# A fused convolution and linear attention: order of the queries' loop, and the planes' edges on VectorE

## The chip, the cores and the metric

The kernel runs on one core of a Trainium2 chip. The metric is the time of one execution on the device in microseconds (us); three runs of the kernel before gave a median of 4165.56 (4163.43 to 4168.52). The engines are TensorE (PE; its weight loads are PEld), VectorE (DVE), ScalarE (ACT), GpSimd (POOL) and SyncE (SP), which issues the DMAs.

## The reference

The input x is (16, 256, 64, 64) in float32. Layer 0 is a group norm and a 3x3 convolution in 8 groups, with weights rotated per batch by an angle that a small network takes from the pooled input, and a modulation per channel. Layer 1 is a group norm and a focused linear attention with 8 heads over the 4096 pixels, with a 5x5 depthwise convolution of the values:

```python
x = x + conv(gn(x), rotated) * sigmoid(mod)
t = tokens(gn(x))
q, k, v = t @ Wq.T + bq, t @ Wk.T + bk, t @ Wv.T + bv
q, k = (relu(q) + 1e-6) / scale, (relu(k) + 1e-6) / scale
q = q ** 3 / norm(q ** 3) * norm(q)              # k likewise; then split into 8 heads
z = 1 / (q @ k.sum(tokens) + 1e-6)
o = (q @ (k.T @ v)) * z + depthwise5x5(v)
x = x + (o @ Wproj.T + bproj)
```

## The kernel before

The program is one loop over the 16 batches b, written out per engine; each engine runs its own list of instructions in order, and counters (semaphores) hold one back until another has done its part. Within a batch come five stages: keys and values (a unit is 512 pixels, a pair is 256 pixels or two tiles of 128; `step_kv`), the state k.T @ v, the depthwise convolution of V (`depthwise`, 32 channels), the 3x3 convolution of batch b + 1 (`convolution`, 8 groups, each in two halves q = 0 and 1 into the two banks of VA), and the queries of batch b (`step_q`). The last two batches are written out apart; the last has no convolution.

**The queries' loop** has NU = 8 units of two pairs, p = 0 and 1. Pair n = 2u + p goes through a chain over all engines:

- TensorE `project` (line 1283, bias 1285) into the bank F[p]; VectorE `floor_max` (809) in place; ScalarE `squares` (1079), two activations with their sums; VectorE `cube` (815) into K3; ScalarE `sixths` (1085); VectorE `ratio` (820, 823); ScalarE `norms` (1091).
- TensorE `transpose_q` (1333) from K3 into the bank T[0]; ScalarE `transposed_q` (1126) copies it to QT; TensorE `attention` (1342) into both banks of VA; VectorE `denominators`, `inverses`, `quotients` (869, 874, 883) into O; GpSimd `add_depthwise` (528).
- TensorE `transpose_o` (1351) into the bank T[1]; ScalarE `high_out` (1130), the high half of O in float16; VectorE `low_out` (899), the rest. With both pairs of a unit there, TensorE `output` (1361) makes both halves of the channels in the banks PP and SM, VectorE `finish` (893) adds the residual, and SyncE stores.

TensorE's step takes its parts of different pairs, in this order:

```python
if live(p):
    pe.wait_ge(f_cube, b * 2 * PAIRS + PAIRS + 2 * u + p + 1)
    project(b, u, p, F, 0)
if live(p - 1):
    transpose_q(b, u - 1 + p, 1 - p)
if live(p - 2):
    attention(b, u - 1, p)
if p == 1 and live(-4):
    for h in range(HALVES):
        output(b, u - 2, h)
if live(p - 3):
    transpose_o(b, u - 2 + p, 1 - p)
```

`live` says whether such a pair exists. `attention` waits for QT of its pair and for the quotients of the pair before; `transpose_o` for O of its pair (o_rdy) and for low_out of the pair before (ol_rdy); `output` for low_out of both pairs of its unit and for `finish` of the unit before. In the same loop SyncE, ScalarE, VectorE and GpSimd take in the next batch (`attn_input`, lines 1070, 803, 519), and in units 8 and 9 TensorE projects the keys and values of its first unit.

**The planes.** The 3x3 convolution reads four planes of 33 x 34 elements per group, whose edges have to be 0. ScalarE `planes` normalises one group's planes in place (1056) and then writes the edges by two activations of 64 x 34 and four of 32 x 32 elements with scale 0 (1061, 1064); the counter cx_rdy tells VectorE `high` (775), which casts the planes to float16, and GpSimd takes the rest (511). Groups 0 to 2 are made during `depthwise`, behind the evacuations (1119) of channels 20, 24 and 28; groups 3 to 7 during `convolution`. There VectorE calls `high` for group g + 3 once the second half of group g is in its bank, ahead of that half's evacuation (792) and statistics (795).

## Time and profile before

| | |
|---|---|
| Runs | 4165.56 us median of 3 (4163.43 to 4168.52) |
| The profiled execution | 4166.2 us, its span 4164.4 us |
| Busy: PE, PEld | 3627.7 us (87%), 2717.4 us (65%) |
| Busy: DVE, ACT, POOL | 2896.2 (70%), 2871.0 (69%), 1394.6 (33%) |
| One batch, middle of the run | 249.2 us, 98.8 of them the queries' loop |
| Largest waits of PE in the loop over batches | for DVE line 830: 59.5 us; for DVE line 899: 54.1; for DVE line 815: 52.4; for ACT line 1119: 47.1 |
| Largest waits of DVE | for ACT line 1064: 288.7 us; for PE line 1264: 243.4; for ACT line 1085: 150.2; for ACT line 1130: 108.9 |
| ACT's edges, all batches | line 1061: 58.9 us in 256 instructions; line 1064: 133.8 us in 512 |

How to read it: busy time is the sum of an engine's instructions, and matmuls are pipelined, so that what a matmul costs its successors is the distance between starts. A row in order of time has the start, the length, engine and line, the operation, out<-in, how many instructions are merged, and in brackets how long the engine was idle before it and what released it. PEclk is the granted clock of TensorE: 1.00 is 2.4 GHz, 0.50 is 1.2 GHz.

### The profile page before, as it was taken

The page shows a single profiled execution, that of the slowest core. Times are in us where ns is not written, and L with a number is a line of the kernel's source. Part 1 is how long each engine was busy: PE and PEld are TensorE (multiplying, and loading weights), DVE is VectorE, ACT ScalarE, POOL GpSimd, SP SyncE. Part 2 cuts the span into 40 slices and gives each one's busy share as a digit, 9 for nine tenths or more (in the row PEclk, how much of TensorE's full clock was granted, in tenths as well). Part 3 has the DMA queues.
Part 4 walks back from the last instruction along what each step waited for, and adds up shares of the span by engine and source line. Part 5 has one row for each costly group of instructions (what it writes and reads, how often), then busy time and mean ns, then how long its engine had stood idle before and what let it go on. Part 6 is the DMA issues. An engine that isn't in the chain of part 4 may idle for free.

```text
span 4164.4 us, 94153 instructions
## 1 busy us (share of the span) xinstructions
PE 3627.7 (87%) x26496; PEld 2717.4 (65%) x26496; DVE 2896.2 (70%) x7633; ACT 2871.0 (69%) x8141; POOL 1394.6 (33%) x1317
## 2 busy tenths in 40 slices
PE   0468999989989988999989989988999989989998
PEld 0155776757667675776757667675766757667676
DVE  6465867768586775867768586785867668585766
ACT  2376776767677676776767677676777767677675
POOL 0441523325133241523325143342523325143311
PEclk9989999999999999999999999999999999999999
DMA  4435434344443435434344443535434344442512
GB/s 164 139 98 155 135 104 132 124 119 141 128 131 107 134 113 155 134 109 135 117 124 140 126 140 96 144 105 154 134 115 137 109 132 132 129 139 59 152 46 72
DMA packets 558467, 516.39 MB, mean 124 GB/s; under 512 B 97296, under 2 KB 491664, under 8 KB 557712
## 3 DMA queue, kind: packets, MB, share of 16 engines
q1 hardware_dynamic: 557968, 510.53, 40.7%
q8 instruction: 217, 3.56, 0.4%
q14 instruction: 282, 2.31, 0.2%
HBM read 351.02 MB, written 134.22 MB: 117 GB/s over the span
## 4 chain that ended last, share of the span: by engine, by line
PE 59%; DVE 16%; issue 11%; ACT 10%; DMA 1%; DVEq 1%; POOL 1%; SPq 1%; ACTq 0%; POOLq 0%
PE VAB L1264 17%; PE F L1283 10%; PE VAB L1283 6%; PE F L1322 5%; PE T L1294 4%; PE VAB L1322 4%; PE SM L1361 4%; PE VAB L1342 2%; ACT WK L1085 2%; ACT WK L1079 2%; DVE WK L830 2%; PE T L1351 2%; DVE F L809 2%; ACT V L1119 2%; PE F L1285 2%
## 5 line engine op out<-in xcount | busy, mean ns | idle before, releaser
L1283 PE MATMUL F<-WQ,XHL 128*128 128x256 f16 x6144 | 814.0, 273 | 47.1 <-DVE XR L792 13.7
L1264 PE MATMUL VAB<-WK,BD 128*128 128x512 f16 x3072 | 724.9, 395 | 103.4 <-DMA BD<-RHL 54.7
L528 POOL TENSOR_TENSOR XR<-XR,V 128x512 f32<-128x512 f32 x256 | 327.5, 1279 | 1226.6 <-DVE XR L883 1226.6
L1079 ACT ACTIVATE WK<-F,SCAL 128x256 f32<-128x256 f32 x1024 | 474.3, 469 | 369.1 <-DVE F L809 368.3
L511 POOL TENSOR_TENSOR WK<-XP,WK 128x1122 f16<-128x1122 f32 x128 | 289.9, 2265 | 1248.1 <-DVE WK L775 1248.1
L1283 PEld LDWEIGHTS F<-WQ,XHL 128*128 128x128 f16 (+1 forms) x6144 | 600.3, 99 | 124.5 <-issue 56.0
L1264 PEld LDWEIGHTS VAB<-WK,BD 128*128 128x128 f16 x3072 | 302.5, 101 | 492.3 <-issue 87.7
L1085 ACT ACTIVATE WK<-WK,SCAL 128x256 f32<-128x256 f32 x1024 | 513.0, 508 | 66.2 <-DVE WK L815 62.7
L809 DVE TENSOR_TENSOR F<-F,FL 128x512 f32<-128x512 f32 x512 | 354.7, 693 | 86.9 <-PE F L1285 85.1
L815 DVE TENSOR_TENSOR WK<-WK,F 128x512 f32<-128x512 f32 x512 | 349.6, 683 | 88.2 <-ACT WK L1079 73.7
L1283 PE MATMUL VAB<-WQ,XHL 128*128 128x256 f16 x3072 | 407.0, 273 | 0.0
L792 DVE SCALAR_TENSOR_TENSOR XR<-VAB,MODC,XR 128x512 f32<-128x512 f32 x256 | 191.7, 749 | 243.8 <-PE VAB L1264 243.4
L1156 ACT ACTIVATE XR<-XR,BPC 128x1024 f32<-128x1024 f32 x128 | 146.9, 1147 | 304.5 <-DVE ST L795 304.3
L1294 PE MATMUL T<-VT,WK 128*128 128x129 f32 x2048 | 295.2, 289 | 66.5 <-DVE WK L830 59.5
L775 DVE CAST WK<-XP 128x1122 f16<-128x1122 f32 x128 | 97.3, 762 | 352.4 <-ACT XP L1064 288.7
L1283 PEld LDWEIGHTS VAB<-WQ,XHL 128*128 (+1 forms) x3072 | 301.4, 98 | 36.3
L1294 PEld LDWEIGHTS T<-VT,WK 128*128 128x128 f32 x2048 | 261.2, 199 | 94.0 <-DVE WK L830 88.8
L519 POOL TENSOR_TENSOR XHL<-XP,XHL 128x512 f16<-128x512 f32 x256 | 291.2, 1139 | 93.2 <-DVE XHL L803 93.2
L1342 PE MATMUL VAB<-KVS,VT 128*128 128x132 f32 x2048 | 300.0, 292 | 21.2 <-DVE XR L883 16.4
L1322 PE MATMUL F<-V,TP 128*128 128x248 f16 (+1 forms) x2304 | 297.5, 286 | 14.1 <-ACT V L1119 14.1
L1342 PEld LDWEIGHTS VAB<-KVS,VT 128*128 128x128 f32 x2048 | 261.3, 197 | 52.2 <-DVE XR L883 46.7
L1285 PE MATMUL F<-BQ,ONES 128*128 128x256 f16 x1024 | 279.8, 273 | 0.0
(185 smaller groups left out, 7128.2 us busy)
## 6 DMA issues: line engine op xcount, KB each, us to landing
XR<-xr SPq DMA_DIRECT2D x256, 512.0 KB, 4.9
XP<-xp SPq DMA_DIRECT2D x128, 561.0 KB, 3.8
x<-XR SPq DMA_DIRECT2D x512, 128.0 KB, 2.1
XP<-x SPq DMA_DIRECT2D x256, 256.0 KB, 3.4
XR<-x SPq DMA_DIRECT2D x256, 256.0 KB, 3.3
out<-XR SPq DMA_DIRECT2D x256, 256.0 KB, 3.0
BD<-RHL SPq DMA_DIRECT2D x256, 96.0 KB, 2.3
XHL<-toeplitz SPq DMA_DIRECT2D x2, 3072.0 KB, 12.8
```

The lines of the kernel that those rows point to most:

```text
L519: g_.tensor_tensor(lo, U[:, u % 3, h].rearrange("p m y x -> p y m x"), hi, ALU.subtract).then_inc(l_rdy, 1)
L528: g_.tensor_tensor(o, o, fm, ALU.add).then_inc(o_rdy, 2)
L809: v.tensor_tensor(f, f, fl, ALU.max).then_inc(f_max, 1)
L815: v.tensor_tensor(K3[:, p, :], K2[:, p, :], F[p][:, :], ALU.mult).then_inc(f_cube, 1)
L1079: a.activation(K2[:, p, ts], F[p][:, ts], ACT.Square, scale=inv_a, accum_out=S2[:, 2 * p + t:2 * p + t + 1]).then_inc(f_sq, 1)
L1085: a.activation(K2[:, p, t * C:(t + 1) * C], K3[:, p, t * C:(t + 1) * C], ACT.Square, scale=inv_a, accum_out=S6[:, 2 * p + t:2 * p + t + 1] ...
L1264: ins = t_.matmul(VA[q], BD[:, j, HALVES * wa + h, sx, P * sy:P * (sy + 1)], SG[:, g % 3, xa, 16 * q + sy:16 * q + sy + 16, sx:sx + 32], s ...
L1283: t_.matmul(o, XHL[:, xa, h, at], WQ[:, wa, h, c0:c0 + C], start=(k == 0), stop=False)
L1285: ins = t_.matmul(o, ONES[:, :], BQ[:, c0:c0 + C], start=False, stop=True)
L1294: ins = t_.matmul(T[h][:, 0:P + 1], K3[:, p, t * C + h * P:t * C + (h + 1) * P], VT[:, p, t, h, 0:P + 1], start=False, stop=False)
L1322: ins = t_.matmul(bank[:, lo:hi], TP[:, c, d, ta, :], V[:, c, va, lo + sh:hi + sh], start=(k == 0), stop=(k == 8))
L1342: ins = t_.matmul(VA[t][:, h * KVC:(h + 1) * KVC], QT[:, p, h, t * P:(t + 1) * P], KVS[:, h, :], start=True, stop=True)
```

## The change

Three engines get another order in `step_q`, and VectorE makes the edges of the planes.

- TensorE: attention, transposes of O, projection (or keys of the next batch), transposes of Q; then output of unit u - 2, if p = 0 instead of p = 1. Values of the next batch come last in both steps of unit 9.
- VectorE: denominators, inverses and quotients of pair n - 2 come first, then floor and ratio, low_out of pair n - 3 (was n - 4), both finishes of unit u - 2 at p = 1 (was one per step, of unit u - 3), cube.
- ScalarE: high_out of pair n - 3 comes first in each step (was both of a unit in steps with p = 0); squares, norms, transposed_q, attn_input and sixths keep their order.
- The edges: the six activations are gone from `planes`; `high` waits for the normalised planes (cx_main), issues six memsets and waits for them (cx_rdy).

```diff
@@ VectorE
             def high(c, g):
-                dve.wait_ge(cx_rdy, GROUPS * c + g + 1)
+                dve.wait_ge(cx_main, GROUPS * c + g + 1)
+                s = g % 3
+                for p in range(2):
+                    v.memset(XG[64 * p:64 * p + 64, s, 32 * p, :], 0.0).then_inc(cx_rdy, 1)
+                for p in range(4):
+                    v.memset(XG[32 * p:32 * p + 32, s, 1 - p // 2:33 - p // 2, 32 * (p % 2)], 0.0).then_inc(cx_rdy, 1)
+                dve.wait_ge(cx_rdy, 6 * (GROUPS * c + g + 1))
...
             def step_q(b, u, p, live, nxt, keys=False, fresh=False):
                 n = b * 2 * PAIRS + PAIRS + 2 * u + p
-                if live(p - 4):
-                    low_out(b, u - 2, p)
+                if live(p - 2):
+                    denominators(b, u - 1, p)
+                    inverses(b, u - 1, p)
+                    quotients(b, u - 1, p, fresh and u == 1 and p == 0)
                 if live(p) or keys:
                     floor_max(n, p)
...
-                if live(-6):
-                    finish(b, u - 3, p)
-                if live(p - 2):
-                    denominators(b, u - 1, p)
+                if live(p - 3):
+                    low_out(b, u - 2 + p, 1 - p)
+                if p == 1 and live(-4):
+                    for h in range(HALVES):
+                        finish(b, u - 2, h)
                 if live(p) or keys:
                     cube(n, p)
-                if live(p - 2):
-                    inverses(b, u - 1, p)
-                if live(p - 2):
-                    quotients(b, u - 1, p, fresh and u == 1 and p == 0)
@@ ScalarE
-                act.wait_ge(cx_main, GROUPS * c + g + 1)
-                for p in range(2):
-                    edge = XG[64 * p:64 * p + 64, s, 32 * p, :]
-                    a.activation(edge, edge, ACT.Copy, scale=0.0)
-                for p in range(4):
-                    edge = XG[32 * p:32 * p + 32, s, 1 - p // 2:33 - p // 2, 32 * (p % 2)]
-                    ins = a.activation(edge, edge, ACT.Copy, scale=0.0)
-                ins.then_inc(cx_rdy, 1)
...
-                if p == 0 and live(-4):
-                    high_out(b, u - 2, 0)
+                if live(p - 3):
+                    high_out(b, u - 2 + p, 1 - p)
                 if live(p) or keys:
                     squares(n, p)
...
-                if p == 0 and live(-3):
-                    high_out(b, u - 2, 1)
@@ TensorE
-            def step_q(b, u, p, live):
+            def step_q(b, u, p, live, nxt):
+
+                if live(p - 2):
+                    attention(b, u - 1, p)
+                if live(p - 3):
+                    transpose_o(b, u - 2 + p, 1 - p)
                 if live(p):
                     pe.wait_ge(f_cube, b * 2 * PAIRS + PAIRS + 2 * u + p + 1)
                     project(b, u, p, F, 0)
+                elif nxt and u == NU:
+                    keys(b + 1, 0, p)
                 if live(p - 1):
                     transpose_q(b, u - 1 + p, 1 - p)
-                if live(p - 2):
-                    attention(b, u - 1, p)
-                if p == 1 and live(-4):
+                if p == 0 and live(-4):
                     for h in range(HALVES):
                         output(b, u - 2, h)
-                if live(p - 3):
-                    transpose_o(b, u - 2 + p, 1 - p)
+                if nxt and u == NU + 1:
+                    if p == 0:
+                        pe.wait_ge(o_rdy, 2 * PAIRS * (b + 1) + O_CR)
+                        carry(pe)
+                    values(b + 1, 0, p)
```

The first place is TensorE in a unit in the middle of the queries' loop. T<-MATS,WK are the transposes of Q, T<-MATS,XR those of O, VAB<-KVS,VT is attention, PP and SM are output; an ISA or REGISTER_ALU row is an instruction that only carries a wait. Before, second step of a unit from its projection on:

```order
L1283 MATMUL F<-WQ,XHL 128x256 [waits f_cube]
...
L1330 REGISTER_ALU [waits f_cube]
L1333 MATMUL T<-MATS,WK 128x128 [waits qt_rdy]
...
L1339 ISA [waits qt_rdy]
L1342 MATMUL VAB<-KVS,VT 128x132 [waits z_rdy]
...
L1361 MATMUL PP<-XR,WP 128x512 [waits y_rdy]
...
L1351 MATMUL T<-MATS,XR 128x128 [waits ol_rdy,o_rdy]
```

And now, a step with p = 0:

```order
L1333 ISA [waits qt_rdy]
L1336 MATMUL VAB<-KVS,VT 128x132 [waits z_rdy]
...
L1345 MATMUL T<-MATS,XR 128x128 [waits ol_rdy,o_rdy]
...
L1277 MATMUL F<-WQ,XHL 128x256 [waits f_cube]
...
L1327 MATMUL T<-MATS,WK 128x128 [waits qt_rdy,f_cube]
...
L1351 ISA [waits ol_rdy]
L1355 MATMUL PP<-XR,WP 128x512 [waits y_rdy]
```

The attention and the transposes of O have moved from behind the projection to ahead of it, and output stands last, ahead of the next step's attention.

The second place is ScalarE in the same units: XR<-T is high_out, WK<-F squares, NORM norms, VT<-T the copy to QT, XP attn_input, WK<-WK sixths. Before, a step with p = 0, from its high_out to that of the step's end:

```order
L1130 ACTIVATE XR<-T,SCAL 128x2x256 [waits ot_full]
...
L1079 ACTIVATE WK,S<-F,SCAL 128x256 [waits f_six]
...
L1091 ACTIVATE NORM<-RATIO,SCAL 128x2 [waits f_ratio]
L1126 COPY VT<-T 128x512 [waits cube_used]
...
L1130 ACTIVATE XR<-T,SCAL 128x2x256 [waits ot_full]
L1085 ACTIVATE WK,S<-WK,SCAL 128x256 [waits f_cube]
```

And now, a step:

```order
L1127 ACTIVATE XR<-T,SCAL 128x2x256 [waits ot_full]
...
L1073 ISA [waits f_cube,f_max]
L1076 ACTIVATE WK,S<-F,SCAL 128x256 [waits f_six]
...
L1088 ACTIVATE NORM<-RATIO,SCAL 128x2 [waits f_ratio]
L1123 COPY VT<-T 128x512 [waits cube_used]
...
L1082 ACTIVATE WK,S<-WK,SCAL 128x256 [waits f_cube]
```

One high_out stands ahead of the squares in every step; the copy to QT stands behind the squares of the next pair, as before.

## Rows read from the trace of the kernel before

**Rows 1.** PE, PEld, DVE, ACT, POOL busy by stretch of one queries' loop; clock, DMA
```profile
1144.99:1154.63 9.64, 6.68 (x54) 5.21 (x55) 5.89 (x24) 6.94 (x19) 0.00 (x0) 1.00 0.44 125
1154.63:1229.11 74.48, 69.66 (x517) 54.41 (x515) 63.06 (x182) 55.43 (x174) 28.80 (x24) 0.98 0.43 124
1229.11:1243.75 14.64, 10.90 (x68) 6.70 (x68) 12.92 (x25) 9.78 (x25) 8.29 (x8) 1.00 0.58 172
```

**Rows 2.** TensorE in order of time (start, length, instruction), in the same loop
```profile
1170.92 1.46 PE L1361 MATMUL PP<-XR,WP 128*128 128x512 f16 x6
...
1173.51 0.60 PE L1351 MATMUL T<-MATS,XR 128*128 128x128 f32 x4
...
1193.28 0.60 PE L1351 MATMUL T<-MATS,XR 128*128 128x128 f32 x4
...
1193.72 0.82 PE L1283 MATMUL F<-WQ,XHL 128*128 128x256 f16 x6
...
1195.69 1.07 PE L1342 MATMUL VAB<-KVS,VT 128*128 128x132 f32 x8
...
1196.59 0.60 PE L1351 MATMUL T<-MATS,XR 128*128 128x128 f32 x4
...
1203.24 0.60 PE L1351 MATMUL T<-MATS,XR 128*128 128x128 f32 x4
```

**Rows 3.** All engines in order of time; in brackets the idle time before, and releaser
```profile
1153.46 0.57 ACT L1126 COPY VT<-T 128x512 f32<-128x512 f32 x1
...
1154.17 0.63 PE L1333 MATMUL T<-MATS,WK 128*128 128x128 f32 x4 [2.06 <-ACT VT L1126]
...
1195.59 0.69 DVE L809 TENSOR_TENSOR F<-F,FL 128x512 f32<-128x512 f32 x1
...
1196.40 0.47 ACT L1079 ACTIVATE WK<-F,SCAL 128x256 f32<-128x256 f32 x1 [1.51 <-DVE F L809]
...
1196.63 0.74 DVE L893 SCALAR_TENSOR_TENSOR XR<-PP,SCAL,XR 128x512 f32<-128x512 f32 x1
...
1197.31 0.29 ACT L1091 ACTIVATE NORM<-RATIO,SCAL 128x2 f32<-128x2 f32 x1
...
1197.50 0.58 ACT L1126 COPY VT<-T 128x512 f32<-128x512 f32 x1
...
1236.30 0.73 DVE L899 SCALAR_TENSOR_TENSOR XR<-T,SCAL,XR 128x512 f16<-128x512 f32 x1
...
1237.18 0.63 PE L1351 MATMUL T<-MATS,XR 128*128 128x128 f32 x4 [3.47 <-DVE XR L899]
...
1246.31 0.83 PE L1283 MATMUL F<-WQ,XHL 128*128 128x256 f16 x6 [0.67 <-issue]
...
1248.04 0.70 DVE L809 TENSOR_TENSOR F<-F,FL 128x512 f32<-128x512 f32 x1 [1.13 <-PE F L1285]
```

**Rows 4.** Waits of two engines over the span (total, times, longest); depthwise's end, convolution
```profile
DVE XR L899 <- ACT XR L1130: 108.9, 129, 2.5
...
PE F L1322 <- ACT V L1119: 14.1, 30, 0.7
...
1096.63 1.01 ACT L1119 ACTIVATE V<-VAB,DWB,SCAL 128x256 f32<-128x256 f32 x2
...
1098.22 7.14 PE L1264 MATMUL VAB<-WK,BD 128*128 128x512 f16 x24 [3.13 <-ACT V L1119]
...
1127.52 5.50 PE L1264 MATMUL VAB<-WK,BD 128*128 128x512 f16 x24
```

**Rows 5.** A fill on VectorE in the setup; small instructions beside GpSimd in the convolution
```profile
1.66 0.28 DVE L573 MEMSET KVS<- 128x264 f32 x1
...
1106.49 2.32 POOL L511 TENSOR_TENSOR WK<-XP,WK 128x1122 f16<-128x1122 f32 x1 [7.07 <-DVE WK L775]
...
1107.79 1.04 DVE L699 TENSOR_TENSOR GS<-GS 128x8 f32<-128x8 f32 x1
```

**Rows 6.** TensorE behind a longer wait, early in the queries' loop
```profile
1163.99 0.71 PEld L1333 LDWEIGHTS T<-MATS,WK 128*128 128x128 f32 x4 [2.80 <-ACT VT L1126]
```

More of the change, by code:

```diff
@@ L1141, in step_q @@
                     norms(n - 1, 1 - p, den_eps)
+                    transposed_q(b, u - 1 + p, 1 - p)
                 elif keys:
                     norms(n - 1, 1 - p, inv_a2)
-                if live(p - 1):
-                    transposed_q(b, u - 1 + p, 1 - p)
                 if nxt:
                     attn_input(b + 1, u - 3, p)
-                if p == 0 and live(-3):
-                    high_out(b, u - 2, 1)
                 if live(p) or keys:
@@ L1414, in batch @@
                     for p in range(2):
-                        if not last and u == NU:
-                            keys(b + 1, 0, p)
-                        if not last and u == NU + 1 and p == 1:
-                            pe.wait_ge(o_rdy, 2 * PAIRS * (b + 1) + O_CR)
-                            carry(pe)
-                            values(b + 1, 0, 0)
-                        step_q(b, u, p, alive(u))
+                        step_q(b, u, p, alive(u), not last)
                         if not last and u == 0:
                             (group_mean, group_spread)[p](b + 1, 1)
-                if not last:
-                    values(b + 1, 0, 1)
             pe.wait_ge(ready, 1)
```

## Prediction

> **What bounds the kernel now.** I read the busy time by stage first, then TensorE's order of time in the queries' loop, then who waits for whom. In the loop's middle TensorE is busy 69.66 of 74.48 us, VectorE 63.06 [rows 1]. TensorE's records end later than they free the engine, so a better reading is its starts: one unit of the loop (two pairs of query tiles) goes from the transposes of O at 1193.28 to the same at 1203.24, 9.96 us [rows 2], and between them TensorE hardly stops. VectorE's only standing wait is the one for ScalarE's high part of O (line 899 behind line 1130), 108.9 us in all [rows 4]. So TensorE and VectorE are both nearly full, and the loop is quick because each engine finds the other's result ready. In such a loop the order on each queue is what counts, since each engine takes its instructions in order.
>
> **What the change moves.** Call step k = 2u + p. Before, TensorE's step was project(k), transpose Q(k-1), attention(k-2), output if p = 1, transpose O(k-3). So while ScalarE was still making QT of pair k-2, TensorE projected pair k. Now the step is attention(k-2), transpose O(k-3), project(k), transpose Q(k-1), output if p = 0. ScalarE keeps its order: squares(k) stands ahead of the copy QT(k-1), as the rows of order show. That closes a ring: attention(k-2), then project(k), whose bank VectorE floors, then ScalarE's squares(k), the norms, the copy QT(k-1), and only then attention(k-1). Nothing in it can run ahead, as each link is behind the one before it on its queue or waits for it.
>
> **The ring's length**, link by link:
> - attention to the transposes of O, start to start: 1196.59 - 1195.69 = 0.90 [rows 2];
> - those to the projection: 1193.72 - 1193.28 = 0.44 [rows 2];
> - projection to VectorE's floor: 1248.04 - 1246.31 = 1.73 [rows 3];
> - floor to squares: 1196.40 - 1195.59 = 0.81 [rows 3];
> - squares to norms 0.91, norms to copy 0.19 (starts 1196.40, 1197.31, 1197.50) [rows 3];
> - copy to the TensorE instruction that waits for it: 1154.17 - 1153.46 = 0.71 [rows 3].
>
> Sum 5.69 us for a step without output. VectorE's denominators, inverses and quotients, which now stand ahead of the floor, end about 2.3 us after the attention starts and the floor can start at 3.07, so they hide.
>
> In a step with p = 0, output stands between this ring and the next attention, and it waits for the low part of pair k-3, which VectorE makes in the same step after floor and ratio. Attention to floor is 0.90 + 0.44 + 1.73 = 3.07; floor to the instruction behind ratio 1196.63 - 1195.59 = 1.04 [rows 3]; low part to the TensorE instruction that waits for it 1237.18 - 1236.30 = 0.88 [rows 3]; two outputs 1173.51 - 1170.92 = 2.59 [rows 2]. Sum 7.58. A unit therefore takes 5.69 + 7.58 = 13.27 us in place of 9.96. TensorE stands still in it for about 5.69 - 3.30 = 2.4 us and once more for some 1.7 us.
>
> **A batch.** From attention(0) to attention(15) there are 15 steps: 7 with output (7 x 7.58 = 53.1), 7 without (39.8), the first one without transposes of O (5.69 - 0.44 = 5.25), and 1.5 more where VectorE does the small chain of the second group norm. Together 99.6, against 74.48 before [rows 1]: +25.1. The start, 9.64 before [rows 1], loses 0.5, since attention(0) no longer stands behind transposes that wait for QT. The end, 14.64 before [rows 1], gains about 1.5: output of unit 7 now waits within one step for the transposes, ScalarE's part (behind the last sixths) and VectorE's part, and nothing covers it; values of the next batch, which covered it, come behind. My estimate for it is 16.1, with ends of 14.6 and 19. So +26.1 a batch, and 16 batches give **+418 us**.
>
> **The fills.** During the depthwise stage ScalarE made three planes with six small instructions each. The last two evacuations start at 1096.63 and end at 1097.64, and the convolution starts at 1098.22, 3.13 us after TensorE's last matmul, which therefore ended at 1095.09 [rows 4]. Without the fills ScalarE has caught up: one evacuation (0.51) and the same 0.58 of waking remain, so about 1.1 of 3.13; saved 2.0. The waits inside the stage, 14.1 us in all [rows 4], are 0.9 a batch and go too. After the wait the first 24 matmuls take 7.14 instead of 5.50 [rows 4]; behind a wait of 1.1 they should not: 1.6. Together 4.6, for 15 batches **-69 us** (between -30, if the clock falls anyway, and -69).
>
> On VectorE, the nearest row is a memset of 264 elements, 0.28 us [rows 5]; fills of 32 or 34 elements take a third of it or less, six of them with the wait behind them some 0.65. They stand behind the wait for the convolution's second half, ahead of the cast and of the evacuation of bank 1, for which TensorE has another half in hand (5.50 / 2 = 2.75 us [rows 4]): hidden at most groups. At group 2 the small chain of the next batch's group norm follows at once, and the next evacuation was already just in time: 0.65 late, 14 batches, **+9 us** (0 to +45, if all five fills of a batch showed).
> A short VectorE instruction can take longer than its work: line 699 took 1.04 us for 8 elements while GpSimd's line 511 ran until 1108.81 [rows 5]. The Trainium skill (SBUF - State Buffer, Who interferes with whom) says that a VectorE instruction with two inputs in SBUF is blocked for the whole of a GpSimd instruction that reads SBUF, and one with at most one input, outside its two-port modes, is not. By it the fills, which read nothing, stay at their own length, and the sum is as above; if they were held like line 699, the last of them would come 1 us later each time. This trace agrees for line 699; for a fill beside GpSimd no run here shows it.
>
> **The clock.** Behind a wait of 2.52 us the transposes took 1.11 us instead of the 0.63 behind one of 2.06 [rows 3, 6]; yet behind 3.47 they took 0.63 again [rows 3]. So TensorE falls to half clock behind some such waits and not behind others. The new loop has a wait of 2.4 us in each of about 7 units. One fall costs 1.64 us by the convolution's first matmuls [rows 4]. None would be 0, all would be 7 x 16 x 1.64 = 184; I take half, **+92 us**, as 2.4 lies between the wait that did it and the one that didn't.
>
> **Sum.** 4166.2 (the profiled execution's own time, 0.6 above the median of 4165.56) + 418 - 69 + 9 + 92 = **4616 us**, 10.8% slower. Range: the clock takes 92 off or adds 92; the links can each be 0.03 to 0.05 off, 0.2 a step, 15 x 16 x 0.2 = 48 either way; the end of a batch adds up to 45. **4470 to 4770**.
>
> **Rivals.**
> - **VectorE's wait goes and nothing comes in its place** (faster). The low part is now made in the step after the transposes of O, which come early, so the 108.9 us of line 899 [rows 4] would vanish: 4166 - 109 - 69 + 9 = 3997 us. It decides if QT(k-1) is ready before project(k) is needed. What speaks for it is that VectorE works 63 of 74 us; against it, that ScalarE's copy stands behind squares(k) in both kernels. Chance 0.04.
> - **Only half of the ring closes.** If output didn't wait for the low part of its own step, both steps would take about 5.69, a unit 11.38: +1.42 x 7.5 x 16 = 170; 4166 + 170 - 60 = 4276 us. Against it is the wait on ol_rdy ahead of output, for both pairs of the unit, the second of which is k-3. Chance 0.06.
> - **TensorE stays at half clock in the loop.** Its parts of the ring, about 2 x 2.87 + 2.59 = 8.3 us a unit, would double: + 8.3 x 7.5 x 16 = 1000, 5500 us. Each slow stretch in this trace ended by itself under dense work, and the loop keeps TensorE busy over two thirds. Chance 0.03.
> - **It doesn't do what it says.** The order of the built kernel shows the steps moved on TensorE, so there is no case of no change. Near zero.
>
> **Chances.** The forecast has 0.87, the range leaves out the rivals. A difference of 0.2% is about what a measurement of this kernel can tell. Faster 0.04, same 0.01, slower 0.95.
>
> **What would show it.** Right: attention to attention 5.7 and 7.6 us in turn, TensorE's line of attention waiting for ScalarE's copy QT some 2.4 us once a unit and its output waiting for VectorE's low part some 1.7 us; the convolution's start waiting 1.1 us for ScalarE; VectorE's wait for line 1130 gone, one for attention there. Wrong: a unit under 11 us, or attention that finds QT ready.

## The result and the profile after

The changed kernel takes **4685.39 us** (median of 4 runs, 4682.73 to 4687.55), the kernel before 4165.85 beside it: ratio **1.1247**, 95% interval 1.1231 to 1.1264. I had said 4616, range 4470 to 4770. Its profiled execution has a span of 4684.2 us and a mean granted clock of 0.947, against 0.971 before.

The windows of one middle batch (us; busy time and count of PE, PEld, DVE, ACT, POOL; clock; DMA). The stretches are the start of the queries' loop, attention(0) to attention(15), end of the batch, keys and values:
```profile
1237.83:1246.99 9.16, 4.67 (x36) 3.51 (x37) 5.28 (x23) 6.46 (x17) 0.00 (x0) 0.96 0.42 117
1246.99:1350.77 103.78, 75.06 (x531) 58.90 (x532) 66.99 (x185) 58.72 (x180) 30.99 (x26) 0.95 0.33 96
1350.77:1371.39 20.62, 12.23 (x71) 7.62 (x70) 11.19 (x24) 10.18 (x24) 8.44 (x11) 0.83 0.38 111
1371.39:1436.31 64.92, 60.05 (x517) 53.07 (x517) 49.25 (x134) 52.12 (x183) 29.89 (x38) 0.97 0.28 84
```
The start is 9.16 for 9.64, as forecast. The second row answers to the 74.48 of [rows 1]: 29.3 us more, with nearly the same work in it (531 matmuls for 517; TensorE 75.06 busy against 69.66, in part because of half clock). The third answers to the end of a batch: before it was 16.24 from attention(15) to the keys' stage, now 20.62 at a clock of 0.83.

The ring in all engines' order of time (start, length, instruction, idle before and releaser), from attention(k-2) to attention(k-1):
```profile
1308.99 1.06 PE L1336 MATMUL VAB<-KVS,VT 128*128 128x132 f32 x8
1309.89 0.60 PE L1345 MATMUL T<-MATS,XR 128*128 128x128 f32 x4
...
1310.33 0.82 PE L1277 MATMUL F<-WQ,XHL 128*128 128x256 f16 x6
...
1312.06 0.70 DVE L816 TENSOR_TENSOR F<-F,FL 128x512 f32<-128x512 f32 x1 [0.71 <-PE F L1279]
...
1312.88 0.47 ACT L1076 ACTIVATE WK<-F,SCAL 128x256 f32<-128x256 f32 x1 [1.66 <-DVE F L816]
...
1313.79 0.29 ACT L1088 ACTIVATE NORM<-RATIO,SCAL 128x2 f32<-128x2 f32 x1
...
1313.97 0.58 ACT L1123 COPY VT<-T 128x512 f32<-128x512 f32 x1
```
Attention to floor 3.07 us, floor to squares 0.82, squares to norms 0.91, norms to copy 0.18, and 0.71 to the next attention at 1314.68: 5.69, link by link as the prediction has it.

TensorE around it (attention L1336, transposes of O L1345, project L1277, transpose Q L1327, output L1355):
```profile
1301.29 1.16 PE L1336 MATMUL VAB<-KVS,VT 128*128 128x132 f32 x8 [2.23 <-ACT VT L1123]
...
1306.39 1.47 PE L1355 MATMUL PP<-XR,WP 128*128 128x512 f16 x6 [1.54 <-DVE XR L906]
1307.70 1.46 PE L1355 MATMUL SM<-XR,WP 128*128 128x512 f16 x6
...
1314.68 2.12 PE L1336 MATMUL VAB<-KVS,VT 128*128 128x132 f32 x8 [2.23 <-ACT VT L1123]
1316.60 1.06 PE L1345 MATMUL T<-MATS,XR 128*128 128x128 f32 x4
1317.45 1.09 PE L1277 MATMUL F<-WQ,XHL 128*128 128x256 f16 x6
```
Two waits a unit. A step with output takes 7.70 (1301.29 to 1308.99), one without 5.69. The wait of 2.23 is followed once by full clock (1.16; granted clock 1.00 from 1301.29 to 1304.26) and once by half (2.12, and 1.06 and 1.09 behind it, where 0.60 and 0.82 are usual; granted clock 0.50 from 1314.68 to 1317.9). The waits over the span, by TensorE, VectorE and ScalarE (total, times, longest):
```profile
PE VAB L1336 <- ACT VT L1123: 333.6, 144, 3.6
PE PP L1355 <- DVE XR L906: 228.0, 128, 3.8
DVE Z L876 <- PE VAB L1336: 333.2, 163, 3.8
DVE XR L906 <- ACT XR L1127: 14.0, 16, 0.9
```
VectorE's wait for ScalarE's high part, 108.9 us in [rows 4], is down to 14.0, as rival 1 had said; in its place TensorE waits 333.6 us for the copy QT and 228.0 for the low part.

The end of the batch, TensorE:
```profile
1355.77 0.63 PE L1345 MATMUL T<-MATS,XR 128*128 128x128 f32 x4 [1.97 <-DVE XR L906]
1360.16 2.74 PE L1355 MATMUL PP<-XR,WP 128*128 128x512 f16 x6 [3.76 <-DVE XR L906]
1362.69 2.77 PE L1355 MATMUL SM<-XR,WP 128*128 128x512 f16 x6
...
1371.39 0.28 PE L1388 MATMUL T<-NOT,ONES 32*128 32x130 f16 x2 [2.65 <-issue]
1372.41 1.30 PE L1277 MATMUL F<-WQ,XHL 128*128 128x256 f16 x6 [0.74 <-issue]
```
The last output waits 3.76 us and then runs at half clock (2.74 for 1.47; granted clock 0.50 from 1360.2 to 1365.2), and most of the next stage's first projection is at half clock too (1.30 for the 0.83 of [rows 3]).

### The profile page after: what moved, and what is told of

It reads as the page before. It is cut to its first block, busy times and chain, and to the rows that moved or that the text cites. A ratio compares the mean times of both kernels' runs of the same rounds, so it can differ in the third digit from the quotient of the medians.

```text
span 4684.2 us, 94247 instructions
## 1 busy us (share of the span) xinstructions
PE 3734.0 (80%) x26496; PEld 2796.9 (60%) x26496; DVE 2981.2 (64%) x8401; ACT 2702.0 (58%) x7373; POOL 1400.1 (30%) x1317
## 4 chain that ended last, share of the span: by engine, by line
PE 60%; DVE 17%; issue 10%; ACT 9%; DVEq 1%; DMA 1%; POOL 1%; SPq 0%; ACTq 0%; POOLq 0%
PE F L1277 12%; PE VAB L1258 10%; PE VAB L1336 6%; PE F L1316 5%; PE VAB L1277 5%; PE VAB L1316 5%; PE PP L1355 4%; PE SM L1355 4%; ACT WK L1076 4%; PE T L1288 3%; DVE F L816 3%; PE T L1345 2%; PE F L1279 2%; DVE XR L906 2%; DVE XR L799 2%
## 5 line engine op out<-in xcount | busy, mean ns | idle before, releaser
L1277 PE MATMUL F<-WQ,XHL 128*128 128x256 f16 x6144 | 874.6, 286 | 45.8 <-DVE XR L799 13.7
L1258 PE MATMUL VAB<-WK,BD 128*128 128x512 f16 x3072 | 707.9, 386 | 85.3 <-DMA BD<-RHL 54.7
L1277 PEld LDWEIGHTS F<-WQ,XHL 128*128 128x128 f16 (+1 forms) x6144 | 628.7, 103 | 149.3 <-issue 54.8
L1336 PE MATMUL VAB<-KVS,VT 128*128 128x132 f32 x2048 | 322.3, 306 | 333.6 <-ACT VT L1123 333.6
L1258 PEld LDWEIGHTS VAB<-WK,BD 128*128 128x128 f16 x3072 | 291.2, 98 | 466.7 <-DMA BD<-RHL 54.8
L1336 PEld LDWEIGHTS VAB<-KVS,VT 128*128 128x128 f32 x2048 | 288.8, 209 | 382.7 <-issue 325.8
L1277 PE MATMUL VAB<-WQ,XHL 128*128 128x256 f16 x3072 | 410.8, 275 | 0.0
L1355 PE MATMUL PP<-XR,WP 128*128 128x512 f16 x768 | 207.6, 411 | 228.0 <-DVE XR L906 228.0
L1277 PEld LDWEIGHTS VAB<-WQ,XHL 128*128 (+1 forms) x3072 | 305.2, 99 | 43.3 <-issue 7.7
L1127 ACT ACTIVATE XR<-T,SCAL 128x512 f16<-128x512 f32 x256 | 174.0, 680 | 264.7 <-PE T L1345 264.7
L1094 ACT ACTIVATE V<-VAB,SCAL 128x256 f32 (+1 forms) x512 | 214.6, 470 | 139.0 <-PE VAB L1279 133.1
```

Of the source, the lines that this page charges most:

```text
L1258: ins = t_.matmul(VA[q], BD[:, j, HALVES * wa + h, sx, P * sy:P * (sy + 1)], SG[:, g % 3, xa, 16 * q + sy:16 * q + sy + 16, sx:sx + 32], s ...
L1277: t_.matmul(o, XHL[:, xa, h, at], WQ[:, wa, h, c0:c0 + C], start=(k == 0), stop=False)
L1336: ins = t_.matmul(VA[t][:, h * KVC:(h + 1) * KVC], QT[:, p, h, t * P:(t + 1) * P], KVS[:, h, :], start=True, stop=True)
L1355: ins = t_.matmul((PP, SM)[h][:, :], WP[:, wa, kk, h * P:(h + 1) * P], OT[:, xa, kk, :].rearrange("p (y m x) -> p m y x", y=4, m=4), start ...
```

## The experiments

Stages of all kernels, each the mean of the 14 middle batches, worked out from TensorE's starts in the trace of each (us a batch; "times 16" below turns one into a sum over the run; keys includes the end of the state, depthwise runs to the convolution's first matmul, the next column holds the convolution and the start of the queries' loop, end runs from attention(15) to the keys' stage):

| kernel | keys | depthwise | convolution to attention(0) | loop | end | time of the runs, ratio to before |
|---|---|---|---|---|---|---|
| before | 65.2 | 36.9 | 56.2 | 74.4 | 16.0 | 4165 to 4167 |
| changed | 66.5 | 33.8 | 55.7 | 105.7 | 19.9 | 4685.4, 1.1247 |
| fills only | 66.0 | 33.6 | 56.2 | 74.4 | 17.0 | 4140.4, 0.9933 (0.9919 to 0.9946) |
| order only | 66.5 | 36.9 | 55.8 | 104.2 | 19.6 | 4716.3, 1.1319 (1.1301 to 1.1336) |
| copy ahead | 66.8 | 33.1 | 52.8 | 100.5 | 18.9 | 4544.3, 1.0902 (1.0885 to 1.0918) |
| output late | 66.3 | 33.3 | 55.7 | 99.3 | 16.4 | 4528.2, 1.0856 (1.0837 to 1.0874) |
| output late, busy | 66.8 | 33.0 | 55.7 | 90.7 | 14.9 | 4371.1, 1.0497 (1.0478 to 1.0516) |
| attention first | 66.6 | 36.6 | 55.6 | 108.0 | 17.7 | 4740.2, 1.1378 (1.1358 to 1.1399) |
| both first | 65.1 | 36.5 | 55.6 | 98.5 | 16.4 | 4539.9, 1.0889 (1.0870 to 1.0908) |
| new order | 66.5 | 36.7 | 54.2 | 71.6 | 16.1 | 4113.8, 0.9873 (0.9857 to 0.9888) |
| fills early | 66.3 | 33.4 | 55.0 | 74.8 | 16.9 | 4125.4, 0.9889 (0.9873 to 0.9906) |
| new order, early | 67.2 | 33.3 | 52.9 | 72.2 | 15.8 | 4051.5, 0.9724 (0.9710 to 0.9737) |
| fills, busy end | 65.4 | 33.1 | 56.2 | 74.5 | 16.0 | 4114.4, 0.9872 (0.9855 to 0.9889) |
| new, early, busy end | 66.9 | 33.2 | 52.9 | 72.5 | 15.2 | 4032.7, 0.9682 (0.9665 to 0.9698) |

**The two halves apart.** Fills only: the kernel before, with the changed kernel's `high` and `planes`. Order only: the changed kernel with `high` and `planes` of before.

> The kernel before, with the edges of the planes filled by VectorE and no order changed. My theory: what ScalarE gets back in the depthwise stage is the prediction's -69 (4.6 us a batch), and the fills, six of which the changed kernel's trace shows to take 0.96 us from the first to the cast, cost VectorE nothing but at the group with the small chain: +9 to +15. So 4166 - 69 + 9 to 15 = 4106 to 4115 us, the convolution starting 1.1 to 1.2 us after the last depthwise copy is waited for. Rival: in the convolution VectorE is the engine waited for, so that every one of five groups comes 1 us later: the gain would be at most 2.0 to 4.6 - 5 x 0.96 = about 0, 4155 to 4170 us.

> The changed kernel, with the edges back on ScalarE as before: the order alone. If the parts add up, it is slower than the changed kernel by what the fills gain, 50 to 70 us: 4735 to 4755 us, 1.137 to 1.142 of the time before; the loop of queries takes 103.8 us a batch as in the changed kernel. Rival: part of the gain of the fills is taken back by a clock that falls elsewhere, then under 30 us between them: 4700 to 4715 us.

Fills only gives -27, half of what I expected; order only is 31 above the changed kernel, about the rival's figure of under 30: its loop is 1.5 us a batch shorter than the changed kernel's, where the clock falls more often. So the loss is the order's alone, and the fills are worth 27 to 31, not 60. The table says where the rest went: depthwise gives 3.3 us a batch (2.9 forecast), but the convolution takes as long as before, although its first matmuls no longer run at half clock, and end and keys take 1.8 more. The convolution in fills only, TensorE:
```profile
1105.33 8.26 PE L1262 MATMUL VAB<-WK,BD 128*128 128x512 f16 x36 [0.20 <-DVE XR L798]
1113.86 0.39 PE L1228 MATMUL SM<-SB,MATS 128*128 128x8 f32 x2 [0.26 <-DVE SB L718]
1114.56 2.85 PE L1262 MATMUL VAB<-WK,BD 128*128 128x512 f16 x12 [0.32 <-DVE XR L798]
1117.60 2.85 PE L1262 MATMUL VAB<-WK,BD 128*128 128x512 f16 x12 [0.20 <-DVE XR L798]
```
and its VectorE:
```profile
1096.91 0.24 DVE L775 MEMSET XP<- 64x34 f32 x2 [1.31 <-PE VAB L1262]
1097.23 0.61 DVE L777 MEMSET XP<- 32x32 f32 x4
1097.87 0.75 DVE L781 CAST WK<-XP 128x1122 f16<-128x1122 f32 x1
```
The six fills and the step to the cast take 0.96 us (1096.91 to 1097.87), and TensorE waits for VectorE's evacuations at several groups. Over the span the wait of the convolution for the evacuation is:
```profile
PE VAB L1262 <- DVE XR L798: 12.4, 44, 2.1
```
In the kernel before it is 1.3 us, one time.

**Fills early.** Only the place of the fills is new; `edges(c, g)` holds the six of a group:
```diff
                         v.bn_stats(ST[:, 1, g, q, :], tile).then_inc(s1_rdy, 1)
+                        if q == 0 and g + 3 < GROUPS:
+                            edges(c, g + 3)
```


> The kernel with only the fills on VectorE, but each group's fills behind the statistics of the first half of the group three earlier, where TensorE has another half to do, instead of ahead of the cast. The run with the fills alone gained 27 us where I expected 51 to 60; its trace starts the convolution 3.3 us earlier, has 5.51 us for the first 24 matmuls, and yet ends the stage no sooner: TensorE waits 0.2 to 0.3 us for VectorE's evacuations at several groups. My theory: those waits are the fills' 0.96 us ahead of cast and evacuation; off that chain the convolution gets its 1.6 us a batch back: 4110 to 4120 us, and the stage from its first matmul to the first attention 54.5 to 55.0 in place of 56.2. Rival (the fills' work itself is too much for VectorE there, or the loss is the clock's): the stage stays at 56.0 to 56.4 and the time at 4135 to 4145 us.

The stage fell to 55.0, as forecast, and the wait above is down from 12.4 to 4.7 us. The time, 4125, is 5 over the range (two of the five runs lie in it): the loop took 0.4 and the keys 0.3 us a batch more. So the fills ahead of the cast cost 1.2 us a batch. That is the first half of what was missing.

**Busy end.** The other half should be the clock. In the kernel before, the wait of 3.47 at a batch's end is followed by full clock [rows 3], in all 13 middle batches that have it (the 14th waits 3.22, and its clock falls in both kernels). In fills only, the same wait in the same place is followed by half clock in 10 of the 13. One of them:
```profile
1230.25 0.63 PE L1349 MATMUL T<-MATS,XR 128*128 128x128 f32 x4 [3.46 <-DVE XR L905]
...
1231.48 1.46 PE L1281 MATMUL VAB<-WQ,XHL 128*128 128x256 f16 x6
1232.73 0.42 PE L1283 MATMUL VAB<-BQ,ONES 128*128 128x256 f16 x1
1232.94 2.43 PE L1359 MATMUL PP<-XR,WP 128*128 128x512 f16 x6
```
The second projection and most of the output are at half clock (granted clock 0.54 from 1231.5 to 1235.2; it is 1.00 behind the wait in the kernel before). The kernel "fills, busy end" fills that wait (the result is read by nobody):
```diff
+                if u == NU + 1 and p == 0:
+                    pe.wait_ge(qt_rdy, b * PAIRS + PAIRS + QT_CR)
+                    for _ in range(26):
+                        t_.matmul(T[0][:, 0:C], ONES[:, :], BQ[:, 0:C], start=True, stop=True)
```


> The run with the fills alone, plus 26 matmuls of 256 columns whose result nobody reads, ahead of the last transposes of O of a batch, where TensorE waits 3.46 us for VectorE. In the kernel before that wait is followed by full clock, in the run with the fills alone by half clock in most batches, though it is as long; the end of the batch took 0.96 us more and the keys' stage 0.82 more. My theory (the fills' gain was given back as falls of the clock there): with TensorE busy in the wait the end of a batch is back at 16.0 or less, 1.0 to 1.8 us a batch less: 4111 to 4125 us. Rival (the loss there is not the clock's, or the fall only moves to the next wait): 4135 to 4145 us.

```profile
1220.57 3.00 PE L1369 MATMUL T<-BQ,ONES 128*128 128x256 f16 x26
1224.21 0.63 PE L1349 MATMUL T<-MATS,XR 128*128 128x128 f32 x4 [0.64 <-DVE XR L905]
```
4114.4: another 26 us gone, the end back at 16.0. TensorE has more work and the kernel is faster; behind the shorter wait its rows are at full clock (granted clock 1.00 from 1224.2 to 1228.5) in all 14 batches. With it the fills are worth 50 us, near the 60 of the prediction (whether the same matmuls would help the kernel before, whose end is at full clock already, was not run). In [rows 4] the convolution's first matmuls were at half clock; the edit took that fall away, and falls came at the end of the batch. Why the end's wait is followed by full clock in one kernel and mostly by half in the other, no run tells.

**The ring, link by link.** Copy ahead changes one place of ScalarE in the changed kernel:
```diff
+                if live(p - 1):
+                    transposed_q(b, u - 1 + p, 1 - p)
                 if live(p) or keys:
                     squares(n, p)
                 if live(p - 1):
                     norms(n - 1, 1 - p, den_eps)
-                    transposed_q(b, u - 1 + p, 1 - p)
```


> The changed kernel, with ScalarE's copy QT(k-1) ahead of squares(k) instead of behind its norms: this opens the ring at the link that the prediction names, and leaves TensorE's and VectorE's orders alone. My theory: the step without output goes from 5.69 to about 4.2 us (attention, transposes of O, project, transpose Q, copy, 0.9 + 0.4 + 1.3 + 0.6 + 0.9), the step with output stays at 7.6 to 8.5, because that one waits for the low part of O, so a unit takes 11.8 to 12.7 in place of 13.39: 7.5 x 16 x 0.7 to 1.6 = 84 to 190 us less, 4495 to 4600 us. TensorE's wait for QT is mostly gone, the one for the low part is longer. Rival (the loss is TensorE's own, by the half clock or by order of banks, not by the copy): steps of 5.69 and 7.70 stay and the time stays within 10 us of 4685.

-141 us, inside the range. In the loop the step without output takes 4.22 in every batch, TensorE's wait for the copy falls from 333.6 to 95.3 us, and the wait for the low part grows:
```profile
PE PP L1356 <- DVE XR L906: 298.1, 128, 3.8
PE VAB L1337 <- ACT VT L1123: 95.3, 129, 1.0
```
The step with output has grown from 7.70 to 8.49, or 10.17 where the clock falls behind that wait. So the copy's place behind squares(k) sets the short step, and the low part the long one. The loop gives 5.1 us a batch, 82 of the 141 us. Another 46 come ahead of it: from the first projection to attention(0) a batch takes 6.2 us in place of 9.0, since the first copy no longer stands behind squares either; 16 come at the end.

Output late moves the second link, with a second buffer for the parts of O. TensorE's part is below; VectorE's finish comes one step later too:
```diff
-                if p == 0 and live(-4):
+                if p == 1 and live(-4):
                     for h in range(HALVES):
                         output(b, u - 2, h)
```


> The changed kernel, with output of unit u-2 one step later (end of the step p = 1) and the sums of it in VectorE one step later too; the high and low parts of O get a second buffer. So output no longer waits for a low part of its own step and fills the time in which TensorE waits for QT. My theory: both steps are the ring alone, 5.7 to 5.9 us, a unit 11.4 to 11.7 in place of 13.39, 7.5 x 16 x 1.7 to 2.0 = 204 to 240 us less: 4445 to 4485 us; TensorE's wait for the low part is gone, that for QT 2.2 us only in every second step. If the falls of the clock go with the wait, up to 50 less. Rival (the second wait only takes its share of one that would come anyway, as for the copy): unit over 12.8, less than 70 us gained.

-157 us, less than the 204 forecast. Steps of 5.69 and 5.99 are there as the ring says, and the wait for the low part is gone, but in most units the longer step takes 7.66. TensorE in one of them:
```profile
1268.45 1.66 PE L1336 MATMUL VAB<-KVS,VT 128*128 128x132 f32 x8 [2.23 <-ACT VT L1123]
1269.91 1.06 PE L1345 MATMUL T<-MATS,XR 128*128 128x128 f32 x4
1270.76 1.49 PE L1277 MATMUL F<-WQ,XHL 128*128 128x256 f16 x6
```
The same 2.23 us as in the changed kernel, now followed by half clock (granted clock 0.57 from 1268.45 to 1272.0) in mostly four or five of the six steps with output; in the changed kernel it is one or two of seven. To show that it is the clock, the same kernel with work in that wait:
```diff
+                if p == 0 and live(-1):
+                    pe.wait_ge(z_rdy, 4 * (b * PAIRS + 2 * (u - 1) + 1) + Z_CR)
+                    for _ in range(12):
+                        t_.matmul(VA[0][:, 0:C], ONES[:, :], BQ[:, 0:C], start=True, stop=True)
```


> The run with output late, plus 12 matmuls of 256 columns whose result nobody reads, in the step p = 0 behind transpose Q, where TensorE waits 2.2 us for QT. They add 1.3 us of work to a wait and no work to the path. In the run without them 5 of 7 units a batch had a step of 7.66 instead of 5.99, the rest at half clock. My theory (those steps are the clock's answer to the wait): with the wait under 1 us the steps of 7.66 are gone, a unit takes 5.69 + 5.99 = 11.7, 5 x 1.67 x 16 = 130 us less: 4390 to 4420 us, mean granted clock over 0.96 in place of 0.934. Rival (the longer step has another cause, such as VectorE or a port, or the clock falls whatever TensorE does): 4500 to 4560 us, steps of 7.66 as before.

```profile
1233.43 1.47 PE L1377 MATMUL VAB<-BQ,ONES 128*128 128x256 f16 x12
1235.75 1.17 PE L1336 MATMUL VAB<-KVS,VT 128*128 128x132 f32 x8 [0.84 <-ACT VT L1123]
1236.75 0.60 PE L1345 MATMUL T<-MATS,XR 128*128 128x128 f32 x4
```
-157 us, 19 below the range: steps of 5.61 and 6.00, none of 7.66 from the fourth on, clock 0.969. The loop gives 138 us of it, close to the 130 expected; the end, which I had not counted, gives 23. The falls are the price of the wait, and work that nobody reads buys them off.

**Which move closes the ring.** Attention first is the kernel before with one move on TensorE:
```diff
+                if live(p - 2):
+                    attention(b, u - 1, p)
                 if live(p):
                     pe.wait_ge(f_cube, b * 2 * PAIRS + PAIRS + 2 * u + p + 1)
                     project(b, u, p, F, 0)
                 if live(p - 1):
                     transpose_q(b, u - 1 + p, 1 - p)
-                if live(p - 2):
-                    attention(b, u - 1, p)
```


> The kernel before with one move on TensorE alone: attention(k-2) ahead of project(k) and transpose Q(k-1); output stays where it was, in the step p = 1, so it never waits for a low part of its own step. My theory (the ring closes by this one move): a step without output 5.69 - 0.44 = 5.25 us, a step with output TensorE's own 3.30 + 2.59 = 5.9 us, a unit 11.1 to 11.2 without a fall of the clock, 12.8 with one in every unit (1.66 each, as in the run with output late): 4166 + 7.5 x 16 x 1.2 to 2.9 = 4310 to 4510 us. Rival (it takes both moves to close the ring, attention first alone finds QT ready since ScalarE has a step more): unit 10.0 to 10.4, 4170 to 4220 us.

4740 us, slower than the changed kernel and far above both ranges. It is no ring by ScalarE's copy. VectorE, and TensorE behind it:
```profile
1264.43 0.70 DVE L809 TENSOR_TENSOR F<-F,FL 128x512 f32<-128x512 f32 x1 [6.46 <-PE F L1285]
...
1267.28 0.76 DVE L883 TENSOR_TENSOR XR<-VAB,Z 128x256 f32<-128x256 f32 x2
...
1268.09 1.73 PE L1342 MATMUL VAB<-KVS,VT 128*128 128x132 f32 x8 [2.84 <-DVE XR L883]
```
VectorE has the floor of pair k and its cube ahead of the quotients of pair k-2. As attention(k-2) now precedes project(k), those quotients wait for a projection that they don't need, and the next attention waits for them to free its bank. Both first puts denominators, inverses and quotients ahead of the floor:
```diff
+                if live(p - 2):
+                    denominators(b, u - 1, p)
+                    inverses(b, u - 1, p)
+                    quotients(b, u - 1, p, fresh and u == 1 and p == 0)
                 if live(p) or keys:
                     floor_max(n, p)
```


> The run with attention first on TensorE alone (4740 us, where I had expected 4310 to 4510), and in VectorE the denominators, inverses and quotients of pair k-2 ahead of the floor of pair k, as the changed kernel has them. In that run's trace every step takes 6.39 us: VectorE floors project(k) first, and the quotients that free attention's bank come behind it. My theory: with them first only ScalarE's copy closes the ring: 5.25 us without output, 5.9 with, a unit 11.1 to 11.3, 12.8 with a fall of the clock in each: 4310 to 4510 us, VectorE's quotients no longer waited for by attention. Rival (the order of attention and projection on TensorE costs this much in any company): over 4650 us.

-200 us, 4540. TensorE's attention waits for the copy alone (354.1 us, none listed for the quotients). It is 30 over my range: steps are 5.64 and 6.60 (7.99 with a fall) where I had 5.25 and 5.9, because VectorE's low part now waits 181.9 us for ScalarE's high part ahead of the quotients:
```profile
PE VAB L1340 <- ACT VT L1124: 354.1, 160, 3.6
DVE XR L899 <- ACT XR L1128: 181.9, 203, 2.8
```
So attention first is what closes the ring, and VectorE's move is a repair without which it costs 200 us more. Order only is another 176 us slower than both first. Output in the step of its own low part can be most of that (moving it gave 157 us in output late); the transposes of O ahead of the projection and the new places of the high and low parts were not run apart.

**A version that beats both.** New order keeps project(k) first on TensorE and takes attention(k-2) ahead of transpose Q(k-1), output ahead of the transposes of O; in VectorE the quotients of a unit's second pair stand behind the cube, and the sums of output frame the step p = 0. `ratio` and `attn_input` get other places too, `attn_input` ahead of squares on ScalarE; no run tells these moves apart. The copy's place in ScalarE's step:
```diff
                 if live(p) or keys:
                     squares(n, p)
+                if live(p - 1):
+                    transposed_q(b, u - 1 + p, 1 - p)
+                if p == 0 and live(-3):
+                    high_out(b, u - 2, 1)
                 if live(p - 1):
                     norms(n - 1, 1 - p, den_eps)
```


> The kernel before with the queries' step rearranged in another way: TensorE projects pair k first, as before, then takes attention(k-2), transpose Q(k-1), output, transposes of O; ScalarE copies QT(k-1) right behind squares(k), ahead of the norms; VectorE ends the unit with the quotients of the second pair. Fills stay on ScalarE. My theory (an engine that projects k first has work of its own while QT is being made, so the link that the changed kernel closes stays open, and moving the copy up makes it earlier still): the unit falls from 9.96 to 9.2 to 9.6 us, 7 x 16 x 0.36 to 0.76 = 40 to 85 us less, 4080 to 4127 us. Rival (attention ahead of transpose Q is what costs, wherever the projection stands): QT(k-1) comes later, the unit grows to 10.5 us or more, over 4220 us.

> Both of the two before in one kernel (new order in the queries' loop, fills on VectorE and early). If they add up: 4080 to 4127 less 27 to 55, 4030 to 4095 us, faster than both the kernel before and the changed one. Rival: falls of the clock take back what one of them gains, as they took about half of it in the run with the fills alone: then within 15 us of the better of the two.

New order: -53 us. TensorE's starts in its trace:
```profile
1186.62 1.07 PE L1352 MATMUL VAB<-KVS,VT 128*128 128x132 f32 x8
1187.52 0.60 PE L1343 MATMUL T<-MATS,WK 128*128 128x128 f32 x4
...
1189.92 1.07 PE L1352 MATMUL VAB<-KVS,VT 128*128 128x132 f32 x8
```
Steps of 3.30 and 5.90 in turn, a unit of 9.20 against 9.96 [rows 2], with no wait of TensorE left in its middle. The loop gives 2.9 us a batch and the stretch from the first projection to attention(0) another 2.0 (the copy to QT stands ahead of squares, as in copy ahead); the keys' stage takes 1.4 back. With early fills 4051.5, 62 less, where the fills early alone brought 41. And with the busy end:

> The run with both the new order and the early fills (4051 us), plus the same 26 matmuls in the wait at the end of a batch. Its keys' stage takes 67.2 us a batch against 65.2 of the kernel before, with the same work. My theory: half to all of these 2 us are falls of the clock that the wait brings: 4020 to 4040 us. Rival: the fall moves on to the next wait: 4045 to 4058 us.

4032.7, **0.9682 of the time before**, inside the range; but the keys' stage stayed at 66.9 and the end fell by 0.5 only, so my reason for it holds for a part: the two traces differ by 9 us, the medians by 19, as the trace is one of two runs at 4041 and 4042, with the other three at 4031 to 4033. In the trace the end is at full clock in every batch, but the first projection of the keys takes 2.8 to 3.0 us in 7 of the 14 batches (2.2 to 3.0 in 13 of them without the busy end), where the kernel before has 1.54 in all. In the mean that is 0.7 of the 1.7 us by which the keys' stage is longer here than before; the other 1.0 is open.

## Why the prediction was right or wrong

The forecast case came (10.8% forecast, 12.5% measured). The terms, per batch from the table, times 16, or 15 for the depthwise stage:

- **The ring's length: right.** 5.69 is the measured step to 0.01, and each of its two steps moved when its own link did: copy ahead took the one without output to 4.22, output late the one with output to 5.99 and left 5.69 as it was. The step with output is 7.70 for my 7.58: the transposes of O start 1.00 behind an attention that waited (1301.29 to 1302.29), not the 0.90 that I took from one that hadn't.
- **A batch's loop: right in sum, off in parts.** The steps without any fall add to 6.71 + 6.36 + 7 x 7.70 + 6 x 5.69 = 101.1, where I had 99.6: the first step without its fall is 6.71 (seen in order only; the changed kernel has 7.78 with it), not 5.25. Falls of the clock add 4.5 (105.65 - 101.1), where the term had 92 / 16 = 5.75. Together +31.2 a batch, 499 us, against 402 + 92 = 494.
- **The clock: the size came by luck.** I priced 3.5 falls of 1.64 a batch behind waits of 2.4, 5.75 in all. Falls cost 1.6 where they come, but only one or two come in seven units, 2.8 us a batch. The other 1.75 of the 4.5 are falls in the first two steps, which I had not priced, and the falls at the end and in the keys' stage stood nowhere in the sum. "2.4 lies between the wait that did it and the one that didn't" is no rule: 2.23 is followed by either, and so is 3.46.
- **The end of a batch: mis-sized, the largest miss.** The term was 1.5; measured +3.9 (16.0 to 19.9). My 14.64, 16.1 and 19 count to the last matmul's end, the table to the keys' stage; counted as mine the end is 17.9, inside my bounds, and the step from there to the keys' stage adds 0.7 more. The mechanism (output waits for transposes, high and low part, uncovered) came as described; what I left out is that a wait of 3.76 there puts the outputs at half clock: 5.1 us for both instead of the 2.59 of [rows 2]. +38 us over the term.
- **The keys' stage: missing from the sum.** +1.3 a batch, 21 us: its first projections run at half clock, the first of them 2.4 us in the mean for 1.54 before. Fills only and order only show it each (66.0 and 66.5).
- **The fills: the gain right, the cost not.** Depthwise 3.2 a batch against 2.9; TensorE waits 1.18 at the convolution's start, where I had 1.1. But "hidden at most groups" was the step that failed: six fills take 0.96, not 0.65, because each of these 0.09 us instructions starts 0.15 to 0.18 after the one before, and they stand ahead of a cast and an evacuation that TensorE waits for, in more places than group 2. By the runs above this costs 1.2 us a batch (fills early). From the convolution to attention(0) the sum had -8 - 24 + 9 = -23 us and the table gives -0.5 x 16 = -8: 15 us.
- **Rival 1** was right that VectorE's wait would go, and wrong that nothing would replace it. **Rival 2** is the run with output late: its unit of 5.69 + 5.99 is near the 11.38 of the rival, but with the falls it takes 4528, and 4371 without most of them, not 4276: the first three steps of a batch (7.6, 6.4 and 7.4 us) and the keys' stage (66.8 for 65.2) have their own losses. **Rival 3** did not come.

The misses add to +5 + 38 + 21 + 15, less 4 at depthwise, = +75 us; the measured gap is 4685 - 4616 = 69, as the changed kernel loses less in the first and the last batch (27 and 31 us against 33), which are not in the table's means.

The fill beside GpSimd: the changed kernel's trace has what was missing, VectorE's and GpSimd's rows early in the run:
```profile
116.53 0.24 DVE L776 MEMSET XP<- 64x34 f32 x2
...
116.74 1.40 POOL L488 TENSOR_TENSOR ROT<-ROT,RHL 128x576 f32<-128x576 f32 x1 [0.18 <-POOL RHL L486]
116.86 0.61 DVE L778 MEMSET XP<- 32x32 f32 x4
```
The last four fills lie inside GpSimd's instruction (116.74 to 118.14) and last as long as elsewhere. Of the 768 fills of this trace 93 overlap a GpSimd instruction, 62 for their whole length, and each of them takes 0.085 to 0.087 us, as the others do. By the Trainium skill (SBUF - State Buffer, Who interferes with whom), as the prediction drew on it, an instruction with at most one input in SBUF, outside the two-port modes, is not held: the trace agrees, as far as GpSimd's spans, which are rough, can tell.

## What to carry to other kernels

In a software pipeline over several engines, write down for each engine which item's work stands ahead of which, and walk the loop once: if pair k's projection stands behind pair k-2's attention on one queue, and pair k-1's copy behind pair k's squares on another, the period is the sum of the links, however busy the engines are. Taking the oldest work first is no rule: keep on the engine that is waited for a piece of newer work between producing something and needing it back.

Price a wait of TensorE in two parts: the wait itself, and the half clock that may follow it. Removing one wait can move the fall to another that cost nothing before, so compare falls over a whole batch, and try cheap matmuls that nobody reads in the waits that stay.

## What the runs showed of the hardware

- The same wait in the same place (3.47 and 3.46 us) is followed by full clock in all of 13 batches of one kernel, and by half clock in 10 of 13 of another that differs from it only in the fills, over 100 us earlier. Waits of 2.23 are followed by half clock in one or two of seven steps with output in the changed kernel, in mostly four or five of six with output late.
- TensorE work that nobody reads made kernels faster by 157 us (4528 to 4371), 26 us (4140 to 4114) and 19 us (4051 to 4033).
- Fills of 32 or 34 elements take 0.09 us each but 0.15 to 0.18 from start to start, so six of them and the step to the cast take 0.96; they take no longer inside a GpSimd instruction.
